# Edge stage of a graph attention layer: GpSimd's message product put ahead of its two gathers, behind VectorE's

## The chip, the cores and the metric

The kernel runs on one core of one Trainium2 chip. The metric is the device time of the whole program in microseconds; lower is better. The core has TensorE (matmuls, "PE" in the rows, with its weight loads as "PEld"), VectorE ("DVE"), ScalarE ("ACT"), GpSimd ("POOL"), SyncE ("SP", here only a queue that issues transfers) and 16 DMA engines.

## The reference, cut to what matters

The kernel computes one graph attention layer with a residual, a batch norm over the nodes and a layer norm over each row, all in float32. There are 6250 nodes of width 512, 8 heads of 64, and 106250 edges sorted by destination.

```python
Q = (x @ Wq).reshape(N, H, d); K = (x @ Wk).reshape(N, H, d); V = (x @ Wv).reshape(N, H, d)
score = jnp.einsum('ehd,ehd->eh', K[src], Q[dst]) * scale
score = jnp.exp(jnp.clip(score, -5.0, 5.0))[..., None]
msg = V[src] * score
wV = jax.ops.segment_sum(msg, dst, num_segments=N)
Z = jax.ops.segment_sum(score, dst, num_segments=N)
h = x + (wV / (Z + 1e-06)).reshape(N, D)
# batch norm over the nodes, then: out = layernorm(x + normed)
```

## The kernel before

Three stages follow each other. `project` computes Q, K and V for all nodes and writes them to device memory as `kv_d` (a row of K and V, 4 KB a node) and `q_d`. `attend` is the edge stage, some 1500 of the 2119 us, and the only one that is changed. `normalise` divides, adds and does the two norms.

`attend` goes over 440 **pairs**. A pair is two blocks of 128 edges (`u` = 0 and 1), and an edge has a partition of its own. Pairs rotate through a ring `kv` of 8 slots (`RING`), each with K, V and the 8 weights for both blocks. Each engine has its own queue, written by a function `step(q, s, fills)`, where `q` is the pair and `s = q % 8` its slot; semaphores are the only order between engines. Per pair:

- **GpSimd** fetches the rows of K and V of the source nodes with two indirect DMAs (`gather`, L747), 128 rows of 4 KB each. A gather waits until the pair eight back, which had the slot, has been accumulated (`s_seg`). Once in four pairs it copies indices (L739). It also does the **message product**, V times weight, for one of the eight heads (`weigh`, L710, 128 x 128), with a lag: in its step `q` it issues the gathers of `q` and then the product of `q - 5` (`POOL_LAG`), which waits for ScalarE's exp of that pair (`s_exp`).
- **TensorE** spreads the queries of the destination tile over the edges with one-hot matrices (`q_ps`, L914: four matmuls), one pair ahead of VectorE and only once VectorE has read the pair before (`s_mul`), since `q_ps` has one buffer. In every second step it makes the next one-hot tables (`mm_ps`, L922 and L924). Then it **accumulates** the messages and weights of pair `q - 2` into the destination tile (`acc`, L937), behind `s_v`, which counts the three engines that do message products.
- **VectorE**, in step `q`: clips the scores of `q - 1` (L788), multiplies q·k for pair `q` from `q_ps` and the gathered K (L794), does its message product for `q - 1`, three heads (L710, 128 x 384), and sums q·k by head (L801).
- **ScalarE** turns the clipped scores into weights (exp, L855), does the message product of four heads as eight small activations (L841), turns the one-hot counts into one-hot matrices (L851) and copies a finished destination tile away.
- **SyncE's** queue loads the 512 KB of queries of the next destination tile (L715).

`wait_apart` waits for at least 1 and then for a register's value, on the same semaphore.

Of the kernel before, what the change touches and what calls it, by code (L numbers as in the profile page):

```python
# [58 lines left out]
ACT_HEADS = 4  # L59
POOL_HEADS = 1  # L60
# [565 lines left out]
def attend(nc, block, kv_d, q_d, lb_d, nb_d, xb_d, tabs, agg, rz, kv, first, x_first, s_first, s_slots, soft):  # L626
    lb, nb, q_tile, zeros, less, eps = first
    src_t, bits_row, cnt_row, ident = tabs
    with ExitStack() as ctx:
# [20 lines left out]

        s_g = [soft[f"s_g{s}"] for s in range(RING)]
        s_mul, s_red, s_clip, s_exp = sems("s_mul"), sems("s_red"), sems("s_clip"), sems("s_exp")
        s_v, s_seg = sems("s_v"), [soft[f"s_seg{s}"] for s in range(RING)]

        s_t, s_mm = ([sem(f"{name}{n}") for n in range(RING // 2)] for name in ("s_t", "s_mm"))
# [78 lines left out]
        @block.gpsimd  # L734
        def _(pool):
            def index(q, s, fills):
                last = s + IDX_PAIRS - 1
                wait_apart(pool, s_g[last], 32 * (fills - 1))
                pool.tensor_copy(idx[:, s:last + 1, :].rearrange("p a n -> p (a n)"),  # L739
                                 src_t[:, bass.ds(2 * q, 2 * IDX_PAIRS)]).then_inc(s_idx[s // IDX_PAIRS], 1)  # L740

            def gather(q, s, fills, u):
                if u == 0:
                    if s % IDX_PAIRS == 0:
                        wait_apart(pool, s_idx[s // IDX_PAIRS], fills)
                    wait_apart(pool, s_seg[s], fills - 1)
                pool.indirect_dma_start(kv[:, s, u, 0:2 * DIM], None, kv_d,  # L747
                                        bass.IndirectOffsetOnAxis(idx[:, s, u:u + 1], 0),
                                        bounds_check=N_NODES - 1, oob_is_err=False
                                        ).then_inc(s_g[s], 16)  # L750

            def step(q, s, fills):
                p = q - POOL_LAG
                sp, fp = at(s, fills, -POOL_LAG)
                if there(q):
                    gather(q, s, fills, 0)
                    gather(q, s, fills, 1)
                if there(q + 2) and s % IDX_PAIRS == IDX_PAIRS - 2:
                    index(q + 2, *at(s, fills, 2))
                if there(p):  # L760
                    wait_apart(pool, s_exp[sp], fp)
                    weigh(pool, sp, HEADS - POOL_HEADS, POOL_HEADS).then_inc(s_v[sp], 1)
            pool.wait_ge(soft["s_trc"], 1)
            index(0, 0, 1)

            pool.wait_ge(soft["s_kva"], 16 * (TILES // 2 + 1))
            pool.wait_ge(soft["s_kvb"], 16 * (TILES // 2 + 1))
            for s in range(RING):
                step(s, s, 1)
            with nc.Fori(1, ROUNDS, engines=[pool.engine], head_slot={pool.engine: POOL_HEAD}) as i:  # L770
                for s in range(RING):
                    step(i * RING + s, s, i + 1)
            for q in range(ROUNDS * RING, PAIRS + POOL_LAG):
                step(q, q % RING, q // RING + 1)

        @block.vector
        def _(dve):
            def ready(value):

                return value if isinstance(value, int) else dve.snap(dve.to_reg(value))  # L780

            def step(q, s, fills):

                s1, f1 = at(s, fills, -1)
                gathered, rows_of_q = ready(32 * fills), ready(q + 1)
                if there(q - 1):
                    dve.wait_ge(s_red[s1], f1)
                    dve.tensor_scalar(raw[:, s1, :, :], raw[:, s1, :, :], -5.0, 5.0, ALU.max,  # L788
                                      ALU.min).then_inc(s_clip[s1], 1)
                if there(q):  # L790
                    dve.wait_ge(s_g[s], gathered)
                    dve.wait_ge(s_qx, rows_of_q)
                    k = kv[:, s, :, 0:DIM]
                    dve.tensor_tensor(k, q_ps[:, :, :], k,  # L794
                                      ALU.mult).then_inc(s_mul[s], 1)
                if there(q - 1):
                    dve.wait_ge(s_exp[s1], f1)
                    weigh(dve, s1, ACT_HEADS, HEADS - ACT_HEADS - POOL_HEADS).then_inc(s_v[s1], 1)
                if there(q):
                    dve.wait_ge(s_mul[s], fills)  # L800
                    dve.tensor_reduce(raw[:, s, :, :], heads(kv[:, s, :, 0:DIM]), AX.X,  # L801
                                      ALU.add).then_inc(s_red[s], 1)

            pipeline(dve, step, DVE_HEAD)

            early = slice(0, RZ_EARLY)
            dve.wait_ge(s_evc, RZ_EARLY)
            dve.tensor_scalar(rz[:, early, :], agg[:, early, DIM:AGG], 1e-6, None, ALU.add).then_inc(s_rz, 1)
            dve.wait_ge(s_rz, 1)
            dve.reciprocal(rz[:, early, :], rz[:, early, :]).then_inc(s_rz, 1)  # L810
            dve.wait_ge(s_rz, 2)
            for t in [first_pass(p) for p in range(TILES) if not pool_adds(p)][:SCALED_EARLY]:
                r = rz[:, t, :].unsqueeze(2).broadcast_to([P, HEADS, D_HEAD])
                v = agg[:, t, 0:DIM].rearrange("p (h d) -> p h d", d=D_HEAD)
                dve.tensor_tensor(v, v, r, ALU.mult).then_inc(s_rz, 1)
# [64 lines left out]
        def _(pe):  # L880
# [16 lines left out]
            def step(q, s, fills):  # L897
                a, b, c = q + 3, q + 1, q - 2
                (sa, fa), (sb_, fb), (sc, fc) = at(s, fills, 3), at(s, fills, 1), at(s, fills, -2)
                if there(b):  # L900
                    tiles = []
                    for u in range(2):
                        v = 2 * sb_ + u
                        tile = pe.snap(pe.snap(tile_regs[(v - 1) % PLACES], min_val=0, max_val=TILES - 1)
                                       + bit(2 * s + u), min_val=0, max_val=TILES - 1)
                        pe.reg_mov(tile_regs[v % PLACES], tile)
                        tiles.append(tile)
                    pe.wait_ge(s_mm[sb_ // 2], fb)
                    pe.wait_ge(s_q, 16 * (tiles[1] + 1))
                    wait(pe, s_mul[s], fills if there(q) else 0)  # L910
                    for u in range(2):
                        for n in range(2):
                            part_q = q_tile[:, bass.ds(tiles[u] % 2, 1), n * DIM:(n + 1) * DIM].bitcast(F32R)
                            last = pe.matmul(q_ps[:, u, :], one_hot(sb_, u, 1), part_q, start=(n == 0),  # L914
                                             stop=(n == 1))
                    last.then_inc(s_qx, 1)
                if s % 2 and there(a):
                    pe.wait_ge(s_lb[sa // LB_PAIRS], 16 * fa)
                    m1, f1 = at(s, fills, 1)
                    wait(pe, s_mm[m1 // 2], f1)  # L920
                    for n in range(4):
                        pe.matmul(mm_ps[:, 0, n * P:(n + 1) * P], lb[:, sa + n // 2, n % 2 * P:(n % 2 + 1) * P],  # L922
                                  nb[:, :], start=True, stop=True)
                    pe.matmul(mm_ps[:, 1, :], nb[:, :], lb[:, sa:sa + 2, :], start=True,  # L924
                              stop=True).then_inc(s_t[sa // 2], 1)
                if isinstance(q, int) and q == 0:
                    clear()
                if there(c):
                    tiles = [pe.snap(tile_regs[(2 * sc + u) % PLACES], min_val=0, max_val=TILES - 1)
                             for u in range(2)]  # L930
                    pe.wait_ge(s_v[sc], 3 * fc)
                    pe.wait_ge(s_evict, tiles[1] + 1)
                    for u in range(2):
                        par = tiles[u] % 2
                        m = one_hot(sc, u, 0).bitcast(F32)
                        for n in range(2):
                            last = pe.matmul(acc[:, bass.ds(par, 1), DIM - (1 - n) * HALF:DIM + n * HALF], m,  # L937
                                             kv[:, sc, u, DIM + n * HALF:DIM + (n + 1) * HALF],
                                             start=False, stop=True, skip_group_check=True)
                    last.then_inc(s_seg[sc], 1)  # L940
                if s == RING - 1:
                    fetch(q // RING + 2 if isinstance(q, int) else fills + 1)
# [434 lines left out]
```

## Time and profile before

| | us |
|---|---|
| median of 3 runs | 2110.19 |
| lowest and highest run | 2108.66 and 2122.17 |
| profiled execution, first to last instruction (its span) | 2119.3 |
| of it TensorE matmuls busy | 1935.2 |
| VectorE busy | 1719.8 |
| ScalarE busy | 1377.4 |
| GpSimd busy | 1340.1 |

The profiled execution is one more run of the same program, recorded by the hardware. Only its span is known, from the first to the last instruction; nothing that was recorded lies around it. It is 9.1 us above the median of the runs. Busy times are over the whole span, with all three stages.

### The profile page before, as it was taken

What the parts mean: (1) busy time and instruction counts of PE and PEld (TensorE: products, weight loads), DVE (VectorE), ACT (ScalarE), POOL (GpSimd) and SP (SyncE); (2) the same over time, 40 slices, a digit from 0 to 9 for tenths busy, and PEclk for the clock granted to TensorE, in tenths of its full rate; (3) what the DMA queues carried; (4) which work ended last, traced back from release to release, by engine and by line L of the source; (5) the groups of instructions that cost most, each with busy time, mean ns of one, the idle gap of its engine ahead of it and who ended that gap; (6) DMA issues with size and microseconds to landing.
All of it is one profiled execution on the core that took longest, in us unless ns stands there. A gap on an engine that the chain in (4) does not pass through costs nothing.

```text
span 2119.3 us, 42713 instructions
## 1 busy us (share of the span) xinstructions
PE 1935.2 (91%) x7903; PEld 1358.3 (64%) x8014; DVE 1719.8 (81%) x2454; ACT 1377.4 (65%) x4602; POOL 1340.1 (63%) x1693
## 2 busy tenths in 40 slices
PE   8999999979989989898999999989999898998897
PEld 4555555537666767666666767767767676766433
DVE  6676655538888888888888888889888888888988
ACT  0011000017878878887878888878888887887866
POOL 0106663036777767777777777777777777676657
PEclk9999999999999999999999999999999999999999
DMA  4648886458888888888888889998899898889607
GB/s 172 176 154 301 298 289 233 145 225 273 299 309 302 309 304 303 301 313 310 301 300 320 310 304 315 324 312 305 314 324 318 291 319 314 281 316 320 225 0 288
DMA packets 184521, 589.09 MB, mean 278 GB/s; under 512 B 28480, under 2 KB 30240, under 8 KB 184480
## 3 DMA queue, kind: packets, MB, share of 16 engines
q0 software_dynamic: 135904, 465.14, 63.1%
q1 hardware_dynamic: 45120, 121.69, 16.3%
q10 hardware_dynamic: 3456, 1.78, 0.3%
q8 instruction: 18, 0.29, 0.1%
q14 instruction: 23, 0.19, 0.0%
HBM read 535.27 MB, written 78.91 MB: 290 GB/s over the span
## 4 chain that ended last, share of the span: by engine, by line
PE 67%; DVE 16%; issue 6%; ACT 4%; another core or an unknown queue 3%; DMA 2%; ACTq 1%; SPq 0%; POOL 0%; DVEq 0%
PE acc L937 21%; PE q_ps L914 21%; PE places L342 20%; DVE kv L794 8%; DVE raw L801 3%; ACT kv L841 2%; PE mm_ps L922 2%; DVE stats L1275 1%; DVE agg L1259 1%; DMA q_tile<-q_d 1%; PE places L402 1%; PE mm_ps L924 1%; ACT mm_sb L851 1%; DVE agg L1268 1%
## 5 line engine op out<-in xcount | busy, mean ns | idle before, releaser
L747 POOL DMA_INDIRECT kv<-kv_d,idx x880 | 898.3, 1021 | 505.4 <-issue 178.2
L841 ACT ACTIVATE kv<-kv 128x64 f32<-128x64 f32 x3520 | 888.8, 335 | 14.3
L937 PE MATMUL acc<-kv,mm_sb 128*128 128x260 f32 x3520 | 857.4, 387 | 6.6 <-ACT kv L841 0.6
L937 PEld LDWEIGHTS acc<-kv,mm_sb 128*128 128x128 f32 x3520 | 676.8, 193 | 111.4 <-issue 6.7
L794 DVE TENSOR_TENSOR kv<-q_ps,kv 128x1024 f32<-128x1024 f32 x440 | 537.6, 1222 | 183.4 <-PE q_ps L914 106.0
L914 PE MATMUL q_ps<-q_tile,mm_sb 128*128 x1760 | 546.5, 433 | 144.1 <-DVE kv L794 106.1
L801 DVE TENSOR_REDUCE raw<-kv 128x16 f32<-128x1024 f32 x440 | 532.8, 1211 | 0.0
L914 PEld LDWEIGHTS q_ps<-q_tile,mm_sb 128*128 128x128 f32 x1760 | 318.2, 190 | 290.1 <-issue 246.2
L851 ACT ACTIVATE mm_sb<-mm_ps,less 128x1024 fp32r<-128x1024 f32 x220 | 241.2, 1096 | 26.2 <-issue 13.6
L855 ACT ACTIVATE kv<-raw 128x16 f32<-128x16 f32 x440 | 92.4, 210 | 245.6 <-DVE raw L788 126.6
L710 DVE TENSOR_TENSOR kv<-kv 128x384 f32<-128x384 f32 x440 | 244.8, 556 | 4.0 <-ACT kv L855 2.9
L710 POOL TENSOR_TENSOR kv<-kv 128x128 f32<-128x128 f32 x440 | 181.0, 411 | 22.9 <-ACT kv L855 15.0
L342 PE MATMUL places<-t_sb,s_sb 128*128 128x512 f32 (+1 forms) x552 | 185.5, 486 | 0.0
L435 ACT COPY p<-places 128x768 f32<-128x768 f32 x23 | 18.4, 798 | 247.6 <-PE places L342 247.6
L342 PEld LDWEIGHTS places<-t_sb,s_sb 128*128 128x128 f32 x552 | 104.9, 190 | 73.6 <-issue 66.5
L342 PE MATMUL places<-w_sb,x_sb 128*128 128x512 f32 (+1 forms) x368 | 126.2, 486 | 0.0
L342 PEld LDWEIGHTS places<-w_sb,x_sb 128*128 128x128 f32 x368 | 69.8, 190 | 49.1 <-issue 44.5
L788 DVE TENSOR_SCALAR raw<-raw 128x16 f32<-128x16 f32 x440 | 85.8, 195 | 15.3
L922 PEld LDWEIGHTS mm_ps<-nb,lb 128*128 128x128 bf16 x880 | 51.4, 100 | 63.9 <-issue 63.9
L922 PE MATMUL mm_ps<-nb,lb 128*128 128x128 bf16 x880 | 90.0, 226 | 0.0
L590 DVE TENSOR_TENSOR u<-places,p 128x768 f32<-128x768 f32 x23 | 22.0, 958 | 79.6 <-PE places L342 79.6
L440 ACT COPY kv_a<-places 128x256 f32<-128x256 f32 x23 | 8.5, 371 | 100.0 <-PE places L342 60.2
(171 smaller groups left out, 1357.1 us busy)
## 6 DMA issues: line engine op xcount, KB each, us to landing
q_tile<-q_d SPq DMA_DIRECT2D x49, 512.0 KB
kv<-kv_d,idx POOLq DMA_INDIRECT x880
kv_d<-kv_a SPq DMA_DIRECT2D x25, 512.0 KB
xb<-in_x POOLq DMA_DIRECT2D x49, 256.0 KB, 4.1
xb_d<-xb POOLq DMA_DIRECT2D x49, 256.0 KB, 3.4
out_rows<-agg SPq DMA_DIRECT2D x49, 256.0 KB, 2.1
x_sb<-in_xT SPq DMA_DIRECT2D x24, 512.0 KB, 8.2
q_d<-q_a SPq DMA_DIRECT2D x24, 512.0 KB
```

Of the source, the lines that this page charges most:

```text
L342: last = pe.matmul(out[:, cols], left[:, c, :], right[:, c, cols], start=fresh and c == 0, stop=c == DEEP - 1, skip_group_check=True)
L710: return eng.tensor_tensor(v, v, w, ALU.mult)
L747: pool.indirect_dma_start(kv[:, s, u, 0:2 * DIM], None, kv_d, bass.IndirectOffsetOnAxis(idx[:, s, u:u + 1], 0), bounds_check=N_NODES - 1, ...
L788: dve.tensor_scalar(raw[:, s1, :, :], raw[:, s1, :, :], -5.0, 5.0, ALU.max, ALU.min).then_inc(s_clip[s1], 1)
L794: dve.tensor_tensor(k, q_ps[:, :, :], k, ALU.mult).then_inc(s_mul[s], 1)
L801: dve.tensor_reduce(raw[:, s, :, :], heads(kv[:, s, :, 0:DIM]), AX.X, ALU.add).then_inc(s_red[s], 1)
L841: return act.activation(v, v, ACT.Copy, scale=kv[:, s, u, 2 * DIM + h:2 * DIM + h + 1])
L851: act.activation(mm_sb[:, sa // 2, :, :], mm_ps[:, :, :], ACT.Relu, bias=less[:, 0:1]).then_inc(s_mm[sa // 2], 1)
L855: act.activation(kv[:, s, :, 2 * DIM:KVW], raw[:, s, :, :], ACT.Exp).then_inc(s_exp[s], 1)
L914: last = pe.matmul(q_ps[:, u, :], one_hot(sb_, u, 1), part_q, start=(n == 0), stop=(n == 1))
L922: pe.matmul(mm_ps[:, 0, n * P:(n + 1) * P], lb[:, sa + n // 2, n % 2 * P:(n % 2 + 1) * P], nb[:, :], start=True, stop=True)
L937: last = pe.matmul(acc[:, bass.ds(par, 1), DIM - (1 - n) * HALF:DIM + n * HALF], m, kv[:, sc, u, DIM + n * HALF:DIM + (n + 1) * HALF], sta ...
```

## The change

VectorE's message product no longer counts on the slot's `s_v` but on a semaphore of its own, `s_w`, one for all slots, which grows by one with each pair. GpSimd's step waits for the exp and for `s_w` of pair `q - 5`, does its own message product, and issues the gathers of `q` and the index copy behind it. TensorE waits for two on `s_v` in place of three, and for `s_w`.

```diff
+        s_w = sem("s_w")
...
             def step(q, s, fills):
                 p = q - POOL_LAG
                 sp, fp = at(s, fills, -POOL_LAG)
+                if there(p):
+                    wait_apart(pool, s_exp[sp], fp)
+                    wait_apart(pool, s_w, p + 1)
+                    weigh(pool, sp, HEADS - POOL_HEADS, POOL_HEADS).then_inc(s_v[sp], 1)
                 if there(q):
                     gather(q, s, fills, 0)
                     gather(q, s, fills, 1)
                 if there(q + 2) and s % IDX_PAIRS == IDX_PAIRS - 2:
                     index(q + 2, *at(s, fills, 2))
-                if there(p):
-                    wait_apart(pool, s_exp[sp], fp)
-                    weigh(pool, sp, HEADS - POOL_HEADS, POOL_HEADS).then_inc(s_v[sp], 1)
...
-                    weigh(dve, s1, ACT_HEADS, HEADS - ACT_HEADS - POOL_HEADS).then_inc(s_v[s1], 1)
+                    weigh(dve, s1, ACT_HEADS, HEADS - ACT_HEADS - POOL_HEADS).then_inc(s_w, 1)
...
-                    pe.wait_ge(s_v[sc], 3 * fc)
+                    pe.wait_ge(s_v[sc], 2 * fc)
+                    pe.wait_ge(s_w, c + 1)
```

## Rows read from the trace of the kernel before

**Rows 1.** Stretch of the edge stage: length, each engine's busy us, clock, DMA share, GB/s.

```profile
core 0: us, PE busy (x) PEld busy (x) DVE busy (x) ACT busy (x) POOL busy (x), PEclk, DMA share, GB/s
600.00:1950.00 1350.00, 1223.98 (x5634) 942.04 (x5732) 1175.58 (x1582) 1109.26 (x3850) 986.51 (x1286) 0.98 0.88 309
```

**Rows 2.** The chain of waits, 1276 to 1304 us: start, duration, what.

```profile
1282.98 1.24 DVE kv L794
1284.21 0.30 issue
1284.51 1.18 PE q_ps L914 x4
1285.69 0.24 PE mm_ps L922 x4
1285.93 0.22 PE mm_ps L924
1286.15 1.75 PE acc L937 x8
1287.90 1.65 PE q_ps L914 x4
...
1289.64 1.24 DVE kv L794
```

**Rows 3.** Waits, 600 to 1950 us: us in total, times, longest.

```profile
POOL kv L747 <- remote: 119.1, 122, 1.3
...
DVE kv L794 <- PE q_ps L914: 95.1, 133, 2.1
...
POOL kv L747 <- PE acc L937: 74.4, 57, 4.3
```

**Rows 4.** Instructions of L794, L747 and L710 begun up to 1283.55 us.

```profile
400.00:1283.55 883.55, 290.15 (x238) 0.97 0.85 297
400.00:1283.55 883.55, 492.19 (x482) 0.97 0.85 297
400.00:1283.55 883.55, 131.74 (x236) 96.90 (x236) 0.97 0.85 297
```

**Rows 5.** Timeline of GpSimd: start, duration, what, idle time before and its releaser.

```profile
1283.62 1.02 POOL L747 DMA_INDIRECT kv<-kv_d,idx  x1 [1.03 <-remote]
1284.95 1.00 POOL L747 DMA_INDIRECT kv<-kv_d,idx  x1 [0.30 <-issue]
1285.97 0.41 POOL L710 TENSOR_TENSOR kv<-kv 128x128 f32<-128x128 f32 x1
1286.54 1.02 POOL L747 DMA_INDIRECT kv<-kv_d,idx  x1 [0.16 <-issue]
...
1290.29 1.04 POOL L747 DMA_INDIRECT kv<-kv_d,idx  x1 [0.85 <-remote]
```

**Rows 6.** Timeline of VectorE in the same stretch.

```profile
1284.12 0.55 DVE L710 TENSOR_TENSOR kv<-kv 128x384 f32<-128x384 f32 x1
...
1296.32 1.23 DVE L794 TENSOR_TENSOR kv<-q_ps,kv 128x1024 f32<-128x1024 f32 x1 [0.72 <-PE q_ps L914]
```

**Rows 7.** Timeline of TensorE in the same stretch.

```profile
1288.66 1.92 PE L937 MATMUL acc<-kv,mm_sb 128*128 128x260 f32 x8
```

**Rows 8.** Timelines of ScalarE and GpSimd at the end of the stage.

```profile
1961.43 0.20 ACT L855 ACTIVATE kv<-raw 128x16 f32<-128x16 f32 x1
1961.71 0.40 POOL L710 TENSOR_TENSOR kv<-kv 128x128 f32<-128x128 f32 x1 [2.73 <-ACT kv L855]
```

**Rows 9.** A long piece of the chain; DMA issues (queue, count, KB, us to landing).

```profile
1418.23 4.72 DMA q_tile<-q_d
...
kv<-xb_d SPq DMA_DIRECT2D x6, 1024.0 KB, 8.3
```

**Rows 10.** Instructions of L937: idle time of TensorE before them (us, times).

```profile
issue: 7.1, 23
```

**Rows 11.** VectorE's L710 in the page's groups (busy, mean ns); durations, min/median/max.

```profile
L710 DVE TENSOR_TENSOR kv<-kv 128x384 f32<-128x384 f32 x440 | 244.8, 556 | 4.0 <-ACT kv L855 2.9
L710 DVE TENSOR_TENSOR kv<-kv x440: 541/549/835, 466.1 to 1970.4; 128x384 f32<-128x384 f32 x147
```

## The prediction

> **What bounds the kernel now.** I read the stretch view of the edge stage first. Between 600 and 1950 us TensorE is busy 1224 of 1350 us, VectorE 1176, ScalarE 1109 and GpSimd 987, the 16 DMA engines have a share of 0.88, and the granted clock is 0.98, almost always the higher of the two levels (2.4 GHz) [rows 1]. No engine leaves much room, so busy shares decide nothing here; the order of waits does. The chain of waits shows that order, and in the undisturbed stretch it repeats itself every two pairs: VectorE's product q·k (1.24), 0.30 until TensorE has seen it, the query matmuls of the next pair (1.18), the small matmuls for the one-hot tables (0.24 + 0.22), the accumulation (1.75), the query matmuls of the pair after that (1.65), and then the next q·k, at 1289.64 where the last began at 1282.98 [rows 2]. That is 6.66 us for two pairs, 3.33 for one; 440 pairs at that rate are 1465 us. The reader is to see which names are missing in this loop: GpSimd's message product, the gathers, and VectorE's message product as something that TensorE waits for.
>
> The waits say the same from the other side. GpSimd waits 119.1 us (releaser not named) and 74.4 us for TensorE's accumulation, always ahead of a gather, since a gather may not overwrite its slot before the pair eight back is summed; VectorE waits 95.1 us for the query matmuls [rows 3]. Nobody waits for GpSimd.
>
> Where does each queue stand against the others? Up to 1283.55 us VectorE has begun 238 q·k products, GpSimd has issued 482 gathers (two for a pair) and both have done 236 message products [rows 4]. So the gathers at 1283.62 and 1284.95 are those of pair 241, the GpSimd product at 1285.97 is that of pair 236 and the gather at 1286.54 opens pair 242 [rows 5]; VectorE's product of pair 236 runs from 1284.12 to 1284.67, and its q·k of pair 241 (238, 239 and 240 come between) at 1296.32 [rows 6]. TensorE's accumulation of pair 236 starts at 1288.66 [rows 7].
>
> **The change, part by part.**
> *The order on GpSimd.* Written as a cycle, gather, gather, product is the same cycle before and after, with the same instructions: per pair two gathers, 1283.62 to 1285.95, that is 2.33, a product of 0.41, and 0.16 from the product's end to the next gather if that isn't held up [rows 5]. What changes is which pair the product belongs to: now the product of pair p comes behind the gathers of p+5, after the change ahead of them. No work is added.
>
> *The new wait on GpSimd.* Queued behind it are the product of p, both gathers of p+5 and the index copy. It ends with VectorE's product of p, at 1284.67 in the example. The trace of before has no GpSimd wait for VectorE; the nearest row is GpSimd's product behind ScalarE's exp, which ended at 1961.63 and released it at 1961.71, 0.08 later [rows 8]. So GpSimd's product moves from 1285.97 to about 1284.75, earlier by 1.2. TensorE needs it at 1288.66 [rows 7]: there were 2.3 us to spare and there will be 3.5. Worth nothing, since it was never late.
>
> *The gathers.* Today the gathers of 241 begin at 1283.62, 1.05 ahead of the end of VectorE's product of 236. After the change they begin behind it by 0.08 + 0.41 + 0.16 = 0.65 at least. The other end is a gather that has to be prepared after the wait is over: 0.85 to 1.03 of idle time ahead of those that TensorE released [rows 5], so 0.08 + 0.41 + 1.03 = 1.52. The gathers move later by 1.7 to 2.6 us. I take 2.1, since preparation can run under the 0.41 product in part. What hides this: their q·k is at 1296.32, which is 11.65 behind the end of VectorE's product of 236 [rows 6]. Issue ends 0.65 + 2.33 = 2.98 to 3.85 behind that product, so 7.8 to 8.7 us are left for landing. The trace gives no landing time for gathers. Nearest are the 512 KB query-tile loads of the same stage, as large as one gather and in the same traffic: the longest that the chain waited for took 4.72 us; the other end is a 1024 KB load, as large as both gathers, with 8.3 [rows 9]. I take about 5, for these were measured beside the gathers. So 3 us of cover stay, and the path pays nothing. The slot's own wait (accumulation eight pairs back) is then long over; the 119.1 + 74.4 us of GpSimd's waits [rows 3] become waits for VectorE, which is a change of name and no gain. At the start of the stage only five pairs are gathered without a wait, both before and after, so the start is not touched.
>
> *The new wait on TensorE.* One more wait and one more register step per pair, ahead of the accumulation, behind query matmuls of 1.18 us that are already issued. Accumulations found TensorE idle for want of issue for 7.1 us in 23 cases of 3520 [rows 10]. Lower end 0; upper end the 0.30 that the chain shows between a q·k and the matmuls that it releases [rows 2], which has a wait and address steps in it; only a third of that could be added by one wait, so 0 to 0.1 for a pair, 0 to 44 us. I take 0: the issue is ahead, as the few idle cases say. The semaphore increments on VectorE stay as many as before.
>
> *Collisions of the two products.* VectorE's message product takes 549 ns in the median, 835 at most [rows 11]. The mean is 556, so all of what disturbs it is (0.556 − 0.549) × 440 = 3 us [rows 11]. After the change GpSimd's product starts only when VectorE's is done, and these 3 us can go; VectorE is on the path for half the loop at most, so 0 to 3 gained, and I count 1. The Trainium skill, page "SBUF — State Buffer", section "SBUF: two separate sides", says that VectorE (with two SBUF inputs) and GpSimd share a port pair under an exclusive lock, the later one waiting for the whole instruction. By that rule this change removes a real conflict; the 835 ns agree with it, and the mean says that it is rare today because GpSimd's product lies 1.3 us behind VectorE's.
>
> **Sum.** 0 (order) + 0 (product earlier) + 0 (gathers later, under 3 us of cover) + 0 (TensorE) − 1 (collisions) = −1 us, against a profiled span of 2119.3 us that is 9 above the median of the runs; the sum is a difference and is put to the median: 2109, which I give as 2110.
>
> **The rivals.**
> *1. GpSimd becomes the pace (slower).* GpSimd's place in the step would be product, preparation of the gather in full, two gathers: 0.41 + 0.85 to 1.03 + 2.33 + 0.02 = 3.61 to 3.79 against 3.33. That is 0.28 to 0.46 × 440 = 123 to 202 us: 2233 to 2312. It decides from the point where more than 3.33 − 0.43 − 2.33 = 0.57 us of preparation are exposed in every step, because a queue that stands at VectorE's semaphore can't look ahead. For it: every blocked gather in the trace shows the 0.85 to 1.03 [rows 5]. Against it: two gathers and a product are 2.90 us with what lies between them, under the 3.33 of a pair, so GpSimd has time to see VectorE's semaphore early. Chance 0.10.
>
> *2. The gathers land late (slower).* The cover of 7.8 to 8.7 us is used up where landing takes the 8.3 of the 1 MB load [rows 9]. The loop that then closes runs over five pairs, VectorE's product of p to q·k of p+5, so 0.5 late costs 0.1 a pair, 44 us: 2154. It decides from a landing of 7.8. For it: the DMA share is 0.88 [rows 1]. Against: 4.72 for a load in the same traffic. Chance 0.12. The Trainium skill, "DMA: Bandwidth & Descriptors", section "Rules for kernel authors", advises to issue a transfer early, compute, and wait late; the change does the reverse by 2 us, and by that rule alone this rival would be the result. TensorE's extra wait at its full 0.1 gives the same 44 us; chance 0.05.
>
> *3. TensorE's results reach the others earlier (faster).* In the chain the second query matmuls stand with 1.65 where the first take 1.18, and VectorE waits for them [rows 2, 3]. The trace doesn't say what holds them for 0.47. If it is something that GpSimd does at that moment, the new phase may remove it: 0.47 × 220 = 103 us at most, half of it 52: 2007 to 2058. Against: nothing names GpSimd. Chance 0.13.
>
> **How the numbers follow.** The forecast has 0.60. Its own range is 2095 to 2128. Rivals 1 and 2 with TensorE's wait have 0.27, rival 3 has 0.13. One per cent, 21 us, is about what a measurement can tell from no change. Faster by over 1% is rival 3 and little else, 0.14; slower 0.26; within 1% 0.60. The range leaves out rival 1 and most of rival 3, about 0.2 together: from 2080 to 2160.
>
> **What would show it.** Right: GpSimd's waits ahead of gathers are gone and stand ahead of its product, released by VectorE; its product starts about 0.1 behind VectorE's of the same pair; the two-pair loop is still 6.6 to 6.7 us; no wait of VectorE that a gather ends; VectorE's product never over 0.6 us. Rival 1: GpSimd without any wait, 3.6 us a pair. Rival 2: VectorE idle ahead of q·k with TensorE's query matmuls long done. Rival 3: the 1.65 shrinks to 1.2. The prediction is wrong above all if the late query matmuls hang on GpSimd's phase.

## The result: slower by 4.1%

| | before | after |
|---|---|---|
| median of 4 runs, us | 2116.18 | 2204.1 |
| lowest and highest | 2108.66 and 2126.3 | 2194.57 and 2210.96 |
| profiled span, us | 2119.3 | 2192.8 |
| mean granted TensorE clock | 0.981 | 0.972 |

The ratio is 1.041, 95% interval 1.038 to 1.045: 88 us slower, outside the forecast range of 2080 to 2160.

GpSimd did, in the main, what was foretold. "After" is the changed kernel. These are rows of the page of after (the chain's shares by engine, then groups with busy time, mean ns and idle time before them with its releaser), then the stretch that answers to [rows 1] and the waits that answer to [rows 3].

```profile
PE 47%; DVE 32%; another core or an unknown queue 7%; issue 7%; ACT 3%; DMA 1%; POOL 1%; ACTq 1%; DVEq 0%; SPq 0%; POOLq 0%
...
L748 POOL DMA_INDIRECT kv<-kv_d,idx x880 | 918.4, 1044 | 378.8 <-issue 273.5
...
L711 POOL TENSOR_TENSOR kv<-kv 128x128 f32<-128x128 f32 x440 | 178.7, 406 | 201.1 <-DVE kv L711 188.2
...
L711 DVE TENSOR_TENSOR kv<-kv 128x384 f32<-128x384 f32 x440 | 244.7, 556 | 8.4 <-ACT kv L857 6.1
```

```profile
600.00:1950.00 1350.00, 1183.02 (x5347) 902.13 (x5439) 1117.11 (x1500) 1061.05 (x3650) 951.95 (x1220) 0.97 0.85 293
```

```profile
POOL kv L711 <- DVE kv L711: 149.1, 92, 2.7
DVE kv L796 <- remote: 148.8, 56, 4.4
PE q_ps L916 <- DVE kv L796: 128.3, 56, 4.6
...
DVE kv L796 <- PE q_ps L916: 48.8, 66, 1.7
```

GpSimd now waits for VectorE ahead of its product (149.1 us) and no longer for TensorE ahead of a gather. Its product of a pair and the gathers behind it, in its timeline:

```profile
1286.57 0.41 POOL L711 TENSOR_TENSOR kv<-kv 128x128 f32<-128x128 f32 x1
1287.13 1.03 POOL L748 DMA_INDIRECT kv<-kv_d,idx  x1 [0.16 <-issue]
1288.47 1.00 POOL L748 DMA_INDIRECT kv<-kv_d,idx  x1 [0.31 <-issue]
```

VectorE's product of that pair ran from 1285.59 for 0.55 us, so GpSimd's begins 0.4 behind it; the median over pairs 20 to 429 is 0.44, where about 0.1 was foretold. The first gather begins 1.13 behind VectorE's product in the median, where it was 1.06 ahead: 2.2 us later, 2.1 were forecast. VectorE's product takes 556 ns in the mean, as in [rows 11].

The loss stands elsewhere. VectorE waits 148.8 us for an unnamed releaser ("remote" or "another core or an unknown queue" in the rows; this is a program on one core) and 48.8 for the query matmuls, all ahead of q·k, and TensorE waits 128.3 us for VectorE behind that. The semaphore records give the unnamed one a name. After has 52 pairs of over 5 us, and ahead of each of their q·k the count of the query matmuls is recorded 0.09 us before q·k starts, although the matmuls' row had ended 2.4 to 4.8 us before it. The chain through such a place (start, duration, what), which answers to [rows 2], and TensorE's timeline there, which answers to [rows 7]:

```profile
1278.29 1.92 PE acc L940 x8
1280.21 1.21 PE q_ps L916 x4
...
1281.51 1.23 DVE kv L796
...
1284.45 1.22 DVE kv L796
...
1287.47 2.77 another core or an unknown queue
...
1290.34 1.24 DVE kv L796
1291.58 0.29 issue
1291.87 1.25 PE q_ps L916 x4
```

```profile
1286.13 1.28 PE L916 MATMUL q_ps<-q_tile,mm_sb 128*128 x4
1287.24 1.92 PE L940 MATMUL acc<-kv,mm_sb 128*128 128x260 f32 x8
1291.87 1.25 PE L916 MATMUL q_ps<-q_tile,mm_sb 128*128 x4 [2.71 <-DVE kv L796]
```

The pair that begins at 1281.51 takes 2.94 us, the next one 5.89. The query matmuls for q·k of 1290.34 end by their row at 1287.41, and VectorE starts 2.9 later. TensorE's semaphore counts for these matmuls and for both accumulations beside them are recorded within 0.16 us of each other, at 1290.18 to 1290.34, although their rows end up to 2.7 us apart. So TensorE's counts came behind its rows. What held them isn't in the trace: these groups take 1.3 and 1.9 us each by their rows, so three of them can't all have been worked off in those 0.16 us. The gathers for this q·k had been issued by 1280.38.

Counted from the starts of all q·k: before had 116 pairs of 3.6 to 3.9 us (the long half of the rhythm of two) and 22 of 5 to 9 us; after has 19 and 52. Under 3.2 us there are 247 and 253. So the two-pair rhythm went, and there are twice as many long stops. The sum over all pairs grew from 1505.1 to 1579.2 us, 74.1, which is the whole of the 73.5 by which the span grew.

The stops do not fall at random. With the pairs numbered from 0, 16 of the 23 q·k that end a pair of over 5 us in before (the 22 and one of 10.1 us at the stage's start) have a number that leaves 1 when divided by four; in after 26 of 52 leave 3 and 15 leave 0. So the change moved them to another place of the four-pair pattern of the queues. Which part of that pattern they hang on is not known.

### The profile page after: what moved, and what is told of

Read it like the earlier page. It is cut to its first block, busy times and chain, and to the rows that moved or that the text cites. A ratio compares the mean times of both kernels' runs of the same rounds, so it can differ in the third digit from the quotient of the medians.

```text
span 2192.8 us, 44025 instructions
## 1 busy us (share of the span) xinstructions
PE 1962.3 (89%) x7903; PEld 1368.0 (62%) x8014; DVE 1725.8 (79%) x2454; ACT 1388.7 (63%) x4602; POOL 1360.8 (62%) x1693
## 4 chain that ended last, share of the span: by engine, by line
PE 47%; DVE 32%; another core or an unknown queue 7%; issue 7%; ACT 3%; DMA 1%; POOL 1%; ACTq 1%; DVEq 0%; SPq 0%; POOLq 0%
PE places L342 19%; DVE kv L796 14%; PE acc L940 13%; DVE raw L803 12%; PE q_ps L916 11%; DVE kv L711 2%; ACT kv L843 2%; DVE stats L1278 1%; DVE raw L790 1%; DVE agg L1262 1%; PE places L402 1%; PE mm_ps L924 1%; DVE agg L1271 1%; DMA kv<-kv_d,idx 1%
## 5 line engine op out<-in xcount | busy, mean ns | idle before, releaser
L748 POOL DMA_INDIRECT kv<-kv_d,idx x880 | 918.4, 1044 | 378.8 <-issue 273.5
L940 PE MATMUL acc<-kv,mm_sb 128*128 128x260 f32 x3520 | 874.8, 393 | 13.1 <-issue 7.0
L916 PE MATMUL q_ps<-q_tile,mm_sb 128*128 x1760 | 553.1, 437 | 185.3 <-DVE kv L796 150.0
```

## The experiments

The experiments were run in six groups, on six different chips; which chip the prediction was tested on isn't recorded. The time of the kernel before was not the same on all: 2116 us where the prediction was tested, 1960 on five of the six chips, 2082 on one. I write "the 2116 chip" and "the 2082 chip", and "the 1960 chip" for any of the five; each ratio is against runs of before in the same group. That before differs so much was itself the first finding. None of the six was used twice, so whether the time belongs to the chip or to something that changes from one group to the next isn't shown.

| kernel | gathers of q start, us from the end of VectorE's product of q − 5 | ratio, 1960 chip (95%) | ratio elsewhere |
|---|---|---|---|
| before, again | −1.48 | 0.9998 (0.9988 to 1.0009) | |
| semaphore alone | −1.92 | 1.0032 (1.0023 to 1.0042) | |
| GpSimd's order alone | +0.43 | 1.0028 (1.0016 to 1.0041), 1.0031 (1.002 to 1.0043) | |
| wait, but gathers ahead of it | −1.47 | 1.0050 (1.0033 to 1.0067) | |
| wait, gathers, then product | +1.02 | 1.0199 (1.0182 to 1.0216) | |
| after, again | +1.47 | 1.0106 (1.0084 to 1.0128), 1.0096 (1.0079 to 1.0113) | 1.041 (2116 chip) |
| after, lag 6 | −1.47 | 1.0048 (1.0031 to 1.0065) | 1.0026 (0.9994 to 1.0058), 2082 chip |
| after, lag 4 | +4.46 | 1.0999 (1.097 to 1.1029) | 1.0473 (1.0428 to 1.0518), 2082 chip |

The second column is the median over pairs 20 to 429, from the timelines, on the 1960 chip. −1.48 and −1.92 are not to be told apart: one and the same kernel (before with half of the accumulation left out, below) shows −1.92, −1.93 and −1.48 in its three traces. On the 2116 chip it is −1.06 for before and +1.13 for after; on the 2082 chip −1.22 with lag 6 and +4.45 with lag 4.

### The parts one by one

**Semaphore alone.** GpSimd as before.

```diff
-                    weigh(dve, s1, ...).then_inc(s_v[s1], 1)
+                    weigh(dve, s1, ...).then_inc(s_w, 1)
...
-                    pe.wait_ge(s_v[sc], 3 * fc)
+                    pe.wait_ge(s_v[sc], 2 * fc)
+                    pe.wait_ge(s_w, c + 1)
```

> Only the semaphore changes: VectorE's product counts on a semaphore of its own, TensorE waits for it beside the old one; GpSimd keeps its order and waits for nothing new. Theory A (TensorE's rhythm of 2.94 and 3.75 us by turns, set by GpSimd's gathers that wait for TensorE, is lost): the rhythm is kept, 2116 us +-5. Theory B (where the gathers lie in the pair delays TensorE's results): gathers stay, 2116 +-5. Theory C (the second wait on TensorE costs 0.1 to 0.2 us a pair, 442 pairs): 2160 to 2204.

1965.68 against 1959.29 us. The semaphore and the second wait cost 6 us, 0.015 a pair, and theory C falls for this chip. VectorE's q·k in that run (600 to 1850 us):

```profile
L795 DVE TENSOR_TENSOR kv<-q_ps,kv 128x1024 f32<-128x1024 f32 x396 | 482.8, 1219 | 7.7 <-PE q_ps L915 7.4
```

**GpSimd's order alone**, run twice, with the old semaphore and no wait for VectorE:

```diff
             def step(q, s, fills):
+                if there(p):
+                    wait_apart(pool, s_exp[sp], fp)
+                    weigh(pool, sp, ...).then_inc(s_v[sp], 1)
                 gathers and index as before
-                if there(p): the same product
```

> Only GpSimd's order changes: its product first, then gathers and index; no new semaphore and no wait for VectorE. The gathers begin about 0.4 us later than before (behind the product), not 2.1. Theory A: GpSimd's product no longer stands behind the gathers' wait for TensorE, but the gathers still wait for it; rhythm nearly kept, 2110 to 2140. Theory B: a move of 0.4 of 2.1 us, 2116 to 2135. Theory C: no second wait on TensorE, 2116.

> Only GpSimd's order changed, the old semaphore, no wait for VectorE: the gathers begin 0.4 to 0.7 us behind VectorE's product, between before (-1.4) and the changed kernel (+1.3). Where before takes 2080 or more and the cost follows the start of the gathers step by step: 1.02 to 1.03; where only their gate counts (TensorE's accumulation against VectorE): 1.04, since the product stands ahead of them here too; where before takes 1960: 1.003.

1965.35 and 1967.64. My number for the shift was wrong: the gathers move by 1.9 us and not 0.4, since the product that now stands ahead of them waits for ScalarE's exp. Even so it costs only 6 to 8 us.

**The wait, but behind the gathers**: all of the change except the order of GpSimd's queue.

```diff
                 gathers and index as before
                 if there(p):
                     wait_apart(pool, s_exp[sp], fp)
+                    wait_apart(pool, s_w, p + 1)
                     weigh(pool, sp, ...)
```

> The semaphore and both waits of the change, but GpSimd keeps the order gathers, index, product, with the wait for VectorE's product right ahead of its own product. Theory A: the next gathers stand behind a product that waits for VectorE, so they begin some 1 us later than before; GpSimd no longer waits for TensorE in full: 2116 to 2204, with the long pairs in between (22 before, 52 after). Theory B: gathers between the two kernels in time, 2140 to 2204. Theory C: 2160 to 2204.

1970.32. The gathers stay at −1.47, and the kernel is 11 us over before, 6 of which the semaphore alone costs.

**The wait first, then the gathers, then the product.**

```diff
+                if there(p):
+                    wait_apart(pool, s_w, p + 1)
                 gathers and index as before
                 if there(p):
                     wait_apart(pool, s_exp[sp], fp)
                     weigh(pool, sp, ...)
```

> The semaphore and both waits; GpSimd waits for VectorE's product first, then issues the gathers, then its own product: the gathers begin right behind VectorE's product, 0.5 us earlier than in the changed kernel, and GpSimd's product ends 1 us later. Theory A: the gathers hang on VectorE and no longer on TensorE: like the changed kernel, 2190 to 2210. Theory B: gathers 0.5 us earlier in the pair: 2180 to 2204. Theory C: 2160 to 2204. If it is GpSimd's early product alone that costs: 2116.

1999.46, the dearest of this group, mainly for another reason. GpSimd's product begins 3.46 us behind VectorE's and no longer 0.9, and TensorE's accumulation now stands behind it. Waits of that run:

```profile
PEld acc L941 <- issue: 87.7, 214, 1.7
PE acc L941 <- POOL kv L711: 12.1, 13, 1.5
```

The first line is 11.8 us in the kernel with the wait behind the gathers, and the second has no counterpart there. So a product that had 2.3 us to spare [rows 7] does cost when it is put behind two gathers.

### The two kernels again

> The kernel before, unchanged, for its trace beside the others: ratio 1.00. On the chip of the last call it took 1959 us and not 2116, and the traces there held no pair over 5 us (22 on the first chip). Theory A (TensorE is held back and clocked down on the first chip only, and the two-pair rhythm of 2.94 and 3.75 us is a sign of that): where the time is 1959, under 10 pairs between 3.6 and 3.9 us; where it is 2116, over 100. Theory B (the rhythm is GpSimd's gathers waiting for TensorE): over 100 on either.

> The changed kernel, unchanged. Theory A (the cost is TensorE held back more often): 1.04 on a chip that shows 2116 for before, at most 1.02 on one that shows 1959. Theory B (the gathers' place in the pair costs whatever the chip): 1.04 on either.

> The changed kernel again, to set the other three beside it on this call's chip. Where before takes 2080 or more: 1.04, with some 50 pairs over 5 us and slack of the gathers of 4 us (theory F: TensorE's results come late, more often than before); where before takes 1960: 1.01, with the gathers landing at the last moment in some 50 of 424 pairs (theory G).

1960.11 for before, 1982.58 and 1980.28 us for after: 1.01, as theory G has it and inside theory A's "at most 1.02". The chain of before on this chip (start, duration, what):

```profile
1279.31 1.21 DVE kv L794
1280.52 0.15 DVE kv L710
1280.67 0.23 issue
1280.91 1.22 DVE raw L801
1282.15 0.13 DVE raw L788
1282.28 0.10 issue
1282.38 1.21 DVE kv L794
```

This is another kernel to look at than [rows 2]. From q·k to q·k it takes 3.07 us, and VectorE is alone in it: q·k, its message product, the head sums, the clip. TensorE's matmuls always come in time. No pair lasts over 5 us, six last 3.6 to 3.9, and the sum over all pairs is 1342.6 where the 2116 chip had 1505.1. So the two-pair rhythm of the 2116 chip is no property of the kernel, and theory B's "on either" is refuted. (With lag 6 on the 2082 chip, below, 72 pairs last 3.6 to 3.9 us and 25 over 5.) VectorE's q·k, the idle time before it and its releasers, in before and in after:

```profile
L794 DVE TENSOR_TENSOR kv<-q_ps,kv 128x1024 f32<-128x1024 f32 x397 | 483.4, 1218 | 4.3 <-PE q_ps L914 0.5
```

```profile
L796 DVE TENSOR_TENSOR kv<-q_ps,kv 128x1024 f32<-128x1024 f32 x397 | 483.4, 1218 | 21.0 <-DMA kv<-kv_d,idx 14.3 <-PE q_ps L916 2.7
```

Per q·k that is 4.3/397 = 0.011 and 21.0/397 = 0.053 us; the difference by 440 is 18.6 us, of a difference in span of 1980.9 − 1960.4 = 20.5. Two thirds of it are waits that a gather ends. One of them, VectorE first and then GpSimd's issue for it:

```profile
1110.24 1.22 DVE L796 TENSOR_TENSOR kv<-q_ps,kv 128x1024 f32<-128x1024 f32 x1 [1.25 <-DMA kv<-kv_d,idx]
```

```profile
1100.62 0.40 POOL L711 TENSOR_TENSOR kv<-kv 128x128 f32<-128x128 f32 x1
1101.19 1.18 POOL L748 DMA_INDIRECT kv<-kv_d,idx  x1 [0.16 <-issue]
1102.67 1.00 POOL L748 DMA_INDIRECT kv<-kv_d,idx  x1 [0.30 <-issue]
```

The second gather's issue ends at 1103.67, its last landing is recorded at 1110.22, and q·k starts at 1110.24. On this chip the semaphore record is nearly whole (14059 of 14080 landings in before, 14069 in after). In after the median from the end of issue to the last landing is 5.0 us, the worst 8.3; q·k comes 6.63 us behind the issue (9.58 before). The gathers have a median of 1.50 us to spare where they had 4.51, and 49 of 424 pairs have under 0.3, where before had none.

On the 2116 chip the same record holds only 7151 of 14080 landings in before and 7436 in after, so a last landing can be missing there. The DMA packets settle it, for they are recorded in full on both chips, 144 for each gather. I take the time by which as many packets have ended as all gathers up to a pair have together. On the 1960 chip, where it can be held against the landings, it lies 1.0 us ahead of a pair's last landing in the median and 3.1 at most. In after on the 2116 chip it lies 3.6 us or more ahead of q·k at each of the 49 long stops from pair 16 on, and 5.9 in the median. Late gathers aren't what ends these stops. At 48 of them (pairs 16 to 429) q·k also comes at least 8.9 us behind the end of the gathers' issue, longer than the 8.3 of the slowest landing of this kernel on the 1960 chip.

### The start of the gathers, moved by itself

`POOL_LAG` sets to which pair the product belongs that stands ahead of the gathers. With 6 everything of the change stays, order, semaphore and both waits, but the wait is over a pair earlier, and the slot's own wait sets the gathers' start again. With 4 they start a pair later. GpSimd's product itself hardly moves by this: on the 1960 chip it starts 0.91, 0.90 and 0.34 us behind VectorE's with lag 6, 5 and 4.

```diff
-        POOL_LAG = 5
+        POOL_LAG = 6        (the second kernel: 4)
```

> The changed kernel with GpSimd's product one pair further back (of pair q - 6 in step q). All waits and the order product, gathers, index stay, but the gathers of q now stand behind VectorE's product of q - 6, a pair earlier, so that TensorE's accumulation of q - 8 gates them again, as before the change, some 1.5 us ahead of VectorE's product of q - 5. Theory D (the whole cost is the later start of the gathers): as before, ratio 1.00 +-0.003, and no product waits of GpSimd for VectorE. Theory E (product ahead of the gathers, or the extra wait on TensorE, costs by itself): 1.01, like the changed kernel. Where before takes 2116 us: D gives 2116, E 2204.

> The changed kernel with GpSimd's product one pair nearer (of q - 4 in step q): the gathers of q begin a pair later than in the changed kernel. Theory D: VectorE's product of q - 4 ends three periods less 1.7 us ahead of q.k of q, and the gathers need 1.5 us to start and 7.6 us to land, so a period of 3.6 us: 440 pairs by 0.5 us over before, 2180 us where before takes 1960 (ratio 1.11). Theory E: 1.01.

> The changed kernel with GpSimd's product one pair further back (q - 6), on whichever chip this call comes to. Where before takes 1960 us: the gathers are back at their old place, some 1.5 us ahead of VectorE's product, their smallest slack is over 1 us again, and the ratio is 1.00 to 1.003 (theory D); 1.01 if the order or the second wait costs by itself. Where before takes 2080 or more: 1.003 as seen.

> The changed kernel with GpSimd's product one pair nearer (q - 4). Where before takes 1960 us: the gathers land at the last moment in most pairs. By the median of 7.5 us from a gather's start to its landing, three periods less 1.7 us have to cover 1.5 and 7.5 us: a period of 3.57, 440 pairs by 0.5 us, 2180 (ratio 1.11); by the shift that the first chip bore, 2060 to 2100. Where before takes 2080 or more: 1.047 as seen.

The first two ran on the 2082 chip (2090.12 and 2177.83 us against 2082.24), the others on the 1960 chip (1969.8 and 2159.32 against 1960.05). With the gathers back where they were, TensorE's accumulation gates them again (a wait of lag 6 on the 2082 chip), and what is left of the cost is 0.3 to 0.5%, no more than semaphore and wait cost with the order unchanged:

```profile
POOL kv L748 <- PE acc L940: 54.7, 52, 1.9
```

With lag 4 the idle time before q·k, on the 2082 chip and then on the 1960 chip:

```profile
L796 DVE TENSOR_TENSOR kv<-q_ps,kv 128x1024 f32<-128x1024 f32 x355 | 433.9, 1222 | 181.3 <-DMA kv<-kv_d,idx 110.1 <-issue 24.9 <-remote 22.4
```

```profile
L796 DVE TENSOR_TENSOR kv<-q_ps,kv 128x1024 f32<-128x1024 f32 x353 | 431.3, 1222 | 183.0 <-DMA kv<-kv_d,idx 156.3 <-PE q_ps L916 24.5
```

and with lag 6 on the 1960 chip:

```profile
L796 DVE TENSOR_TENSOR kv<-q_ps,kv 128x1024 f32<-128x1024 f32 x396 | 481.2, 1215 | 7.7 <-PE q_ps L916 7.1
```

Theory D's direction holds on both chips. Its sizes hold for the most part: for lag 6 it gave at most 1.003, and 1.0026 and 1.0048 came, the second a little over; for lag 4 it gave a period of 3.6, and 3.55 and 3.53 came, which makes 1.047 of the ratio where before is slower by itself and 1.10 where it is faster. The two lag 4 kernels are within 19 us of each other although before is 122 us apart: where the gathers set the pace, it no longer matters on which chip.

### Half of TensorE's accumulation left out

Columns 0 to 259 of each message are not summed, in the kernel before and in the changed one. Three pairs of runs, all on the 1960 chip.

```diff
-                        for n in range(2):
+                        for n in (1,):
                             last = pe.matmul(acc[...], m, kv[...])
```

> The kernel before with half of the accumulation left out (columns 0 to 259 of each message are not summed), some 0.9 us less of TensorE per pair. Theory A: TensorE no longer sets the pace, no long holds, VectorE's 2.9 us a pair sets it: 1900 to 1960. Theory B: the phase of the gathers still costs, 1960 to 2060.

> The changed kernel with the same half of the accumulation left out. Theory A: the same as the lightened kernel before within 0.5%. Theory B: 3 to 4% over it.

> The kernel before with half of the accumulation (columns 0 to 259) left out. Theory F (what TensorE has to do is what holds it on the chips where before takes 2080 or more): under 5 pairs over 5 us and the same time as on the other chip, 1945. Rival H (the gathers' traffic holds it, whatever TensorE does): pairs over 5 us stay near 20, 2040 or more.

> The changed kernel with the same half left out. Theory F: 1970, 1.3% over the lightened kernel before, as on the other chip. Rival H: 3 to 4% over the lightened kernel before, with some 50 pairs over 5 us.

> The kernel before with half of the accumulation (columns 0 to 259) left out. Where before takes 2080 or more: theory F (TensorE's own load is what holds it there) 1945 with under 5 pairs over 5 us; rival H (the gathers' traffic holds it, whatever TensorE does) 2040 or more. Where before takes 1960: 1944, as seen.

> The changed kernel with the same half left out. Where before takes 2080 or more: theory F 1970, 1.3% over the lightened kernel before; rival H 3 to 4% over it, with some 50 pairs over 5 us. Where before takes 1960: 1970, as seen.

1944.28, 1943.37 and 1944.76 us against 1970.2, 1969.95 and 1970.01: 1.013 to 1.014 each time. Theory A expected no difference within 0.5% and is refuted for this chip. The cost doesn't shrink when TensorE has a fifth less to do, and the waits say why, before first:

```profile
L794 DVE TENSOR_TENSOR kv<-q_ps,kv 128x1024 f32<-128x1024 f32 x396 | 481.7, 1216 | 1.0 <-PE q_ps L914 1.0
```

```profile
L796 DVE TENSOR_TENSOR kv<-q_ps,kv 128x1024 f32<-128x1024 f32 x396 | 480.9, 1214 | 22.5 <-DMA kv<-kv_d,idx 16.3 <-PE q_ps L916 5.8
```

Of the 22.5 us, 16.3 are waits that a gather's landing ends. What these kernels do on a chip like the first, for which theories F and H were set up, stays untested.

## Why the prediction was wrong, step by step

**The step that failed** is the conclusion of the part on the gathers, "3 us of cover stay, and the path pays nothing", which stands in the sum as 0. On the 2116 chip, where the prediction was tested, the cover did stay (by the packets, 5.0 us in the median over all pairs, or some 4 when the 1.0 by which they run ahead is taken off), and the path paid all the same: 52 pairs of over 5 us in place of 22, and most of the 73.5 us as idle time of VectorE ahead of q·k, behind late counts of TensorE's query matmuls. The sum has no term for that.

The numbers that went into the step: the shift was right (2.1, measured 2.2 on the first chip). The landing was right too ("about 5", measured 5.0 on the 1960 chip), but partly by luck, for the 512 KB query loads that it was taken from have a median of 7.0 us to landing on that chip and 4.72 was one short one.

**On the 1960 chip** it is the cover that was too small. It was worked out as 7.8 to 8.7 us from one place and one rhythm. There a pair takes 3.06 us in before and the gathers move by 2.95; the cover is 6.63 in the median, and the slowest landings take the 8.3 that I held to be only a bound [rows 9]. There rival 2's mechanism is what happens: by the three lags the start of the gathers is worth some 0.5% at +1.5 us and 9.5% at +4.5. It was held unlikely by a median where the late tail decides.

**On the 2116 chip**, where the two kernels differ by 4.1%, the idle time ahead of q·k is 190.0 us before 348 of them between 600 and 1850 us, against 145.1 before 367, which is 0.151 a pair and 66 us of the span's 73.5. The groups of that stretch, before first:

```profile
L794 DVE TENSOR_TENSOR kv<-q_ps,kv 128x1024 f32<-128x1024 f32 x367 | 448.4, 1222 | 145.1 <-PE q_ps L914 87.5 <-remote 52.1 <-issue 4.0
```

```profile
L796 DVE TENSOR_TENSOR kv<-q_ps,kv 128x1024 f32<-128x1024 f32 x348 | 425.2, 1222 | 190.0 <-remote 132.6 <-PE q_ps L916 45.6 <-issue 9.2
```

It is TensorE's counts that are late there ("remote" is the late count described above), not the landing. The prediction named this as what would make it wrong above all, "if the late query matmuls hang on GpSimd's phase", but gave it a price on the faster side only (rival 3) and took for a steady state a rhythm that only this chip has. That the start of the gathers is the cause there too is likely and not shown: the return to no measurable cost with lag 6 was on the 2082 chip, where after itself wasn't run. That trace has 25 pairs of over 5 us, each of them behind a late count of the query matmuls, and 20 of the 25 q·k behind them leave 1 when divided by four, as in before. So with the gathers back at their old place the stops of a slower chip are about as many as in before on the 2116 chip, and fall at the same place of the pattern. That speaks for the start of the gathers, but no trace of before was taken on that chip to set beside it. What is shown is that the cost comes and goes when the lag, and with it little but this start, is moved.

**How a later gather makes TensorE late with 4 us to spare is open.** TensorE's granted clock is part of the picture. Stretches of the long stop shown above, in after:

```profile
1286.00:1289.50 3.50, 3.16 (x15) 2.34 (x13) 1.44 (x3) 3.19 (x11) 3.00 (x5) 1.00 0.93 316
1289.50:1292.90 3.40, 1.03 (x4) 0.69 (x4) 2.56 (x3) 2.08 (x6) 0.57 (x2) 1.00 0.94 333
1292.90:1296.30 3.40, 3.18 (x11) 2.81 (x12) 3.33 (x6) 2.87 (x10) 2.60 (x4) 0.50 0.54 154
```

The lower of the two levels (1.2 GHz) stands in the row behind the stop, where the accumulation takes 3.16 us and not 1.92. In the edge stage, but for its first 10 us, there are 14 such stretches in before and 28 in after. On the 1960 chip there are none in either kernel and 18 with lag 4, where the stops come from landings. Within 3.5 us of the end of a pair of over 5 us begin 14 of the 14, 27 of the 28 and 17 of the 18; but only 14 of 23, 27 of 52 and 17 of 30 such pairs have one behind them, and the lightened kernels have some without any long pair (some ten in one trace of after). So a stop, whatever its cause, often brings the lower clock, and that lengthens what comes behind it; the number of stops is what the change raised.

The Trainium skill, "TensorE: Matmul & The Clock Gate", section "Seeing it yourself", warns that the clock's events in a trace have been seen to be unreliable. If these rows were placed late, the stop itself could be the slow clock. The semaphore counts speak against that. With lag 4 on the 1960 chip all 10 query-matmul and accumulation groups that lie in such rows, and all 23 that end in the 4.4 us before one, count within 0.02 us of the ends of their rows, and the stops there wait for a gather. In after on the 2116 chip 11 of 17 groups in such rows do, and the counts of the rest come 3.6 us later or are missing from the record. So the rows stand where the clock was low. What held TensorE's counts in the stop ahead of them, with 1.00 as the granted clock, stays open.

**The other steps.** GpSimd's product earlier: worth nothing, as foretold; after shows no wait of TensorE for it. TensorE's extra wait: 0 to 0.1 us a pair was given and 0 taken; it is 0.015 with the semaphore alone, 0.3%, on the 1960 chip. Collisions, −1 us: nothing, the mean is 556 ns in both, and the longest still 799. The conflict on the shared port that the Trainium skill describes ("SBUF — State Buffer", section "SBUF: two separate sides") may be gone, but no row shows a gain from it. Rival 1 (GpSimd becomes the pace) fell: it waits 149.1 us for VectorE, and prepares its gathers with 0.16 between product and gather. The Trainium skill's advice in "DMA: Bandwidth & Descriptors", section "Rules for kernel authors", to issue early and wait late, was the better forecast; the lag kernels agree with it, the later start being the dearer on both chips that ran them.

No kernel here that sums everything beats before.

## What to carry to other kernels

A transfer's slack is to be read at its worst landing and at the fastest pair, not at a median and in the rhythm that one profile happens to show. Before a wait is put ahead of a prefetch, work out what gates the prefetch today: a wait that looks like waste (GpSimd's for TensorE) was the earliest start that the ring allows, and a gate on a later event only takes that away. Where one profile shows a rhythm of two with late results, look at a second chip before resting a sum on it.

## What the runs showed of the hardware

- The same kernel took 2116 us where the prediction was tested, 2082 on one chip and 1960 on five, with the first stage alike: 477.6 and 481.5 us of TensorE busy in the first 500 us on the 2116 and the 1960 chip, at a clock of 0.99 and 1.00. The whole difference between these two is in the edge stage (1505.1 and 1342.6 us). On the slower ones VectorE waits for late counts of TensorE; on the 1960 chip VectorE itself is the pace.
- On the 2116 chip TensorE's rows ended 2.8 and, for the accumulation before, 3.7 us ahead of its semaphore counts, which then came in a burst (three within 0.16 us), where a pair took 5.89 us. In both kernels' traces on the 1960 chip the counts stand within 0.05 us of the ends of the rows (1080 and 1081 of 1081 of TensorE's, from 480 us on).
- A semaphore and a wait more on TensorE in each of 440 pairs: 6 us, where VectorE is the pace.
